# Graph attention in steps of four graphs: chunks attended to two slots sooner, and the last step projected in two halves

## The reference

```
h = jnp.maximum(_layernorm(x), 0.0)                 # x: 128 x 128 x 384
q, k, v = split_heads(h @ Wq + bq), split_heads(h @ Wk + bk), split_heads(h @ Wv + bv)
scores = einsum('bhqd,bhkd->bhqk', q, k) / sqrt(32) + beta * adj
scores = where(adj > 0, scores, -9e15)
out = x + einsum('bhqk,bhkd->bhqd', softmax(scores), v)
```

## Time and profile before

| | us |
|---|---|
| median of 3 runs | 978.81 (978.58 to 978.87) |
| the profiled execution's own time | 978.79 |
| its span, first to last instruction | 977.0 |
| PE busy | 953.0 (98% of the span) |
| ACT busy | 900.7 (92%) |
| DVE busy | 896.1 (92%) |
| POOL busy | 799.1 (82%) |

### The profile page before, as it was taken

How to read it: one execution, slowest core, us unless ns; L and a number is a source line. 1 busy time by engine, 2 the same in 40 slices (tenths; PEclk the granted TensorE clock), 3 DMA queues, 4 the chain that set the end, 5 groups by cost and what they waited for, 6 DMA issues and landing times.

```text
span 977.0 us, 33678 instructions
## 1 busy us (share of the span) xinstructions
PE 953.0 (98%) x10607; PEld 666.4 (68%) x10607; DVE 896.1 (92%) x4191; ACT 900.7 (92%) x2397; POOL 799.1 (82%) x998
## 2 busy tenths in 40 slices
PE   5999999999999999999999999999999999999995
PEld 2567667767667777667777667777667777667774
DVE  5899999999999999999999999999999999998887
ACT  7799999999999999999999999999999999999997
POOL 4798888888888888888888888888888888888762
PEclk9999999999999999999999999999999999999999
DMA  6799978998888989888998889999789998977941
GB/s 220 125 183 172 179 166 173 175 169 174 167 181 159 182 172 176 159 187 163 179 170 181 154 179 172 177 170 173 179 168 170 175 170 165 169 155 126 152 126 42
DMA packets 230933, 161.98 MB, mean 166 GB/s; under 512 B 106594, under 2 KB 230756, under 8 KB 230756
## 3 DMA queue, kind: packets, MB, share of 16 engines
q1 hardware_dynamic: 230480, 159.44, 86.3%
q10 hardware_dynamic: 276, 0.40, 0.1%
HBM read 35.52 MB, written 25.17 MB: 62 GB/s over the span
## 4 chain that ended last, share of the span: by engine, by line
PE 82%; issue 3%; POOL 2%; ACT 1%; DVE 1%; POOLq 0%; ACTq 0%; DVEq 0%
PE ps_p L529 49%; PE ps_t L549 15%; PE ps_s L541 8%; PE ps_o L565 3%; PE ps_o L566 3%; PE ps_o L564 3%; ACT probs L632 1%; POOL on L411 1%; DVE biased L764 0%; POOL weighted L387 0%; DVE pT L770 0%; POOL v L405 0%; POOL mask L391 0%; POOL rstd L365 0%; ACT pT L665 0%
## 5 line engine op out<-in xcount | busy, mean ns | idle before, releaser
L632 ACT ACTIVATE probs<-biased,neg_max 128x128 f32<-128x128 f32 x1536 | 490.9, 398 | 26.8 <-DVE neg_max L764 21.8
L529 PE MATMUL ps_p<-hT,w 128*128 128x512 f16 x1728 | 495.7, 379 | 0.2 <-POOL w L469 0.2
L764 DVE CUSTOM_DVE_ANT_0 biased<-ps_s,mask 128x128 f32<-128x128 f32 x1536 | 355.5, 287 | 48.3 <-PE ps_s L541 43.4
L770 DVE TENSOR_TENSOR pT<-ps_t,pT 128x512 f16<-128x512 f32 x384 | 263.5, 686 | 0.7 <-ACT pT L665 0.5
L529 PE MATMUL ps_p<-w,hT 128*128 128x384 f16 x1152 | 248.4, 325 | 0.2 <-POOL w L469 0.2
L549 PEld LDWEIGHTS ps_t<-ident,probs 128*128 128x128 f32 x1536 | 187.4, 140 | 75.5 <-ACT probs L632 22.0
L549 PE MATMUL ps_t<-ident,probs 128*128 128x128 f32 x1536 | 232.3, 274 | 5.5 <-ACT probs L632 5.3
L665 ACT ACTIVATE pT<-ps_t 128x512 f16<-128x512 f32 x384 | 224.5, 585 | 0.6 <-PE ps_o L566 0.6
L541 PEld LDWEIGHTS ps_s<-k_st,q_st 96*128 96x128 f16 x1536 | 117.1, 97 | 78.8 <-issue 1.9
L529 PEld LDWEIGHTS ps_p<-hT,w 128*128 128x128 f16 x1728 | 139.9, 97 | 33.8 <-POOL w L469 2.0
L564 PEld LDWEIGHTS ps_o<-v,pT 128*128 128x128 f16 x1536 | 132.4, 96 | 38.1 <-DVE pT L770 1.2
(11 more groups left out here) (76 smaller groups left out, 1157.8 us busy)
## 6 DMA issues: line engine op xcount, KB each, us to landing
q_st<-qT SPq DMA_DIRECT2D x288, 128.0 KB, 3.6
k_st<-kT SPq DMA_DIRECT2D x288, 128.0 KB, 4.8
out<-on SPq DMA_DIRECT2D x128, 192.0 KB, 3.5
xs<-in_x SPq DMA_DIRECT2D x31, 768.0 KB, 4.6
adjs<-in_adj SPq DMA_DIRECT2D x32, 256.0 KB, 5.5
hT<-h_parts SPq DMA_TRANSPOSE x60, 4.4
k_st<-in_L_gnn_Wk SPq DMA_DIRECT2D x1, 576.0 KB, 5.8
k_st<-in_L_gnn_Wq SPq DMA_DIRECT2D x1, 576.0 KB, 6.9
```

The lines of the kernel that those rows point to most:

```text
L529: mm = pe.matmul(dst, stationary, moving, start=m == 0, stop=m == MMS - 1)
L632: act.activation(probs[:, odd, i, :], biased[:, odd, i, :], ACT.Exp, bias=neg_max[:, odd, i:i + 1], scale=-1.0).then_inc(exp_done, 1)
L764: dve.tensor_tensor_reduce(out=biased[:, odd, i, :], in0=ps_s[:, i * N:(i + 1) * N], in1=mask[:, gp, v // CH, :], scale=-1.0, scalar=3.0e3 ...
L770: dve.tensor_tensor(pT[:, odd, 1], ps_t[odd][:].rearrange("p (h q) -> p h q", q=N), pT[:, odd, 0], ALU.subtract).then_inc(p_low_done, 1)
```

## The change

`LAG` goes from 0 to -2: the slot u of step s now attends to chunk u + 2 of the step before, and slots 10 and 11 to chunks 0 and 1 of their own step. The mask has to be there two slots sooner: POOL makes `weighted` before the last split of tokens and the mask right behind it. There is one transposing DMA for each graph (128 x 6 blocks x 128) in place of one for two. The statistics move one slot later on DVE, and the first sum over the squares of Wv one slot later on PE. The projections of step 31 go in two halves of two graphs (256 columns), spread evenly over 18 slots, so that they reach into step 32. The last graph's output is scaled and added on DVE, one chunk at a time, each from a PSUM bank of its own (`last_outputs`), and stored once.

```diff
-    LAG = 0
+    LAG = -2
...
+    LAST = STEPS - 1
+    HALF = G // 2
+    LAST_UNITS = [unit for g in (0, HALF) for unit in
+                  [("q", c) for c in range(CH)] + [("k", c) for c in range(CH)] + [("v", g + j) for j in range(HALF)]]
+
+    LAST_SLOTS = SLOTS + HALF * CH
...
         def chunk(s, par, u, behind):
 
-            v = u - LAG - behind
-            back = 2 if v < 0 else 1
-            n = SLOTS * (s - 1) + v
-            if v >= SLOTS or (not 0 <= n < CHUNKS):
+            ahead, v = divmod(u - LAG - behind, SLOTS)
+            g = s - 1 + ahead
+            if not 0 <= g < STEPS:
                 return None
-            return n, s - back, par if back == 2 else 1 - par, v % SLOTS
+            return SLOTS * g + v, g, g % 2, v
...
-            def turn_tokens(s, par, half):
-                rows = slice(G // 2 * half, G // 2 * (half + 1))
+            def turn_tokens(s, par, j):
                 wait(sp, proj_done, NB * (s - 1))
                 sp.nop(nofuse=True)
-                sp.wait_ge(h_low, G * (s - 2) + G // 2 * (half + 1))
+                sp.wait_ge(h_low, G * (s - 2) + j + 1)
                 sp.nop(nofuse=True)
-                sp.dma_start_transpose(hT[:, par, rows].rearrange("p j a c t -> p (j a c) t"),
-                                       h_parts[:, rows].rearrange("p j a d -> p (j a d)")).then_inc(hT_in, 16)
+                sp.dma_start_transpose(hT[:, par, j].rearrange("p a c t -> p (a c) t"),
+                                       h_parts[:, j].rearrange("p a d -> p (a d)")).then_inc(hT_in, 16)
...
-                if s == 0 and u in (8, 9):
...
-                ahead, j = {0: (2, 2), 1: (2, 3), 9: (3, 0), 10: (3, 1)}.get(u, (STEPS, 0))
+                ahead, j = {1: (2, 2), 2: (2, 3), 10: (3, 0), 11: (3, 1)}.get(u, (STEPS, 0))
...
+            def last_outputs(c):
+
+                g, j = LAST, G - 1
+                sums = ps_last[c][:, 0:HEADS * VW].rearrange("p (h d) -> p h d", d=VW)[:, c::CH]
+                inv = inv_sum[:, j % 2, c::CH]
+                part = on[:, j % 2, :].rearrange("p (h d) -> p h d", d=HD)[:, c::CH]
+                rest = xb[:, g % 2, j, :].rearrange("p (h d) -> p h d", d=HD)[:, c::CH]
+                dve.wait_ge(pv_done, CH * (G * g + j) + c + 1)
+                wait(dve, scaled, G * g + j - 1)
+                dve.reciprocal(inv, sums[:, :, HD]).then_inc(inverted, 1)
+                wait(dve, stored[j % 2], 16 * (G // 2 * g + j // 2))
+                dve.wait_ge(inverted, G * g + j + c + 1)
+                dve.tensor_tensor(part, sums[:, :, 0:HD], inv.rearrange("p (h o) -> p h o", o=1).broadcast_to([P, HPC, HD]),
+                                  ALU.mult).then_inc(last_scaled, 1)
+                dve.wait_ge(xb_done, G * g + j + 1)
+                dve.wait_ge(last_scaled, c + 1)
+                dve.tensor_tensor(part, part, rest, ALU.add).then_inc(last_added, 1)
```

More of the change, by code:

```diff
@@ L72, in bank_of, with units_of, tokens_of, turn_of @@
         return (NB * s + o) % PB
+    LAST = STEPS - 1
[3 more added lines that the diff above has]
+    LAST_SLOTS = SLOTS + HALF * CH
+    LAST_PIECES = [[] for _ in range(LAST_SLOTS)]
+    last_atoms = [(o, m, D if kind == "v" else HALF * N) for o, (kind, n) in enumerate(LAST_UNITS) for m in range(MMS)]
+    last_total = sum(a[2] for a in last_atoms)
+    done = 0
+    for o, m, cost in last_atoms:
+        runs = LAST_PIECES[(2 * done + cost) * LAST_SLOTS // (2 * last_total)]
+        if runs and runs[-1][0] == o:
+            runs[-1] = (o, runs[-1][1], m + 1)
+        else:
+            runs.append((o, m, m + 1))
+        done += cost
+    def units_of(s):
+        return LAST_UNITS if s == LAST else UNITS
+    def tokens_of(s, o):
+        if s < LAST:
+            return 0, G
+        return (0, HALF) if o < QK + HALF else (HALF, G)
+    def turn_of(s, o):
+        return o if s < LAST or o < QK else o - HALF
+    def pieces_of(s, u):
+        if s < LAST:
+            return s, PIECES[u]
+        slot = SLOTS * (s - LAST) + u
+        return LAST, LAST_PIECES[slot] if slot < LAST_SLOTS else []
+    def ended_in(s, u):
+        if u < 0:
+            s, u = s - 1, u + SLOTS
+        if s < 0:
+            return 0, []
+        of, runs = pieces_of(s, u)
+        return of, [o for o, a, b in runs if b == MMS]
     XB = 4
@@ L265, in _, with spread @@
                 sp.dma_start(xs[:, s], x_v[s]).then_inc(x_in[s], 16)
-            def spread(s, par, kind, c):
+            def spread(s, par, kind, c, half=0):
                 n, src, dst, landed = (0, qT, q_st, q_in) if kind == "q" else (1, kT, k_st, k_in)
@@ L300, in first_step, with last_steps @@
                 sp.dma_start(adjs[:], adj_v[1]).then_inc(adj_in, 16)
+            def last_steps(s, par):
+                if s == LAST:
+                    store(s - 2, 2)
+                    spread(s, par, "q", 0)
+                    spread(s, par, "q", 1)
+                    store(s - 2, 3)
+                    spread(s, par, "q", 2)
+                    for c in range(CH):
+                        spread(s, par, "k", c)
+                    store(s - 1, 0)
+                    store(s - 1, 1)
+                    spread(s, par, "q", 0, 1)
+                    spread(s, par, "q", 1, 1)
+                else:
+                    spread(s - 1, 1 - par, "q", 2, 1)
+                    store(s - 2, 2)
+                    for c in range(CH):
+                        spread(s - 1, 1 - par, "k", c, 1)
+                    store(s - 2, 3)
+                    for j in range(G):
+                        store(s - 1, j)
             def step(s, par):
@@ L370, in split_tokens @@
                 pool.wait_ge(normed, G * s + j + 1)
-                wait(pool, hT_in, 32 * (s - 2))
+                if s > 2:
+                    pool.wait_ge(hT_in, 16 * (G * (s - 3) + j + 1))
                 pool.nop(nofuse=True)
@@ L433, in step @@
                     add_x(s - 2, par, 3)
+                if s == STEPS:
+                    for j in range(HALF, G):
+                        split_v(LAST, 1 - par, j)
                 if masks:
@@ L493, in bank_free @@
                     return
-                before, last = divmod(NB * s + o - PB, NB)
-                kind, n = UNITS[last]
+                before, last = (s, o - PB) if o >= PB else (s - 1, NB + o - PB)
+                kind, n = units_of(before)[last]
                 if kind == "v":
@@ L498, in bank_free @@
                 else:
-                    pe.wait_ge(qk_low, QK * before + last + 1)
+                    pe.wait_ge(qk_low, QK * before + turn_of(before, last) + 1)
             def turn_first(s, bank, c):
@@ L592, in step @@
                         scores(*scored, (u - LAG) % 2)
-                    products = [(o, m) for o, first, end in (PIECES[u] if proj else []) for m in range(first, end)]
+                    of, runs = pieces_of(s, u)
+                    products = [(o, m) for o, first, end in runs for m in range(first, end)]
                     for o, m in products[:2]:
-                        project(s, par, o, m, m + 1)
+                        project(of, of % 2, o, m, m + 1)
                     if turning:
@@ L848, in step @@
                     scored, turned_late, valued = (chunk(s, par, u, behind) for behind in (0, 2, 3))
-                    ended = valued is not None and valued[3] % CH == CH - 1
+                    last = valued is not None and valued[1] == LAST and valued[3] // CH == G - 1
+                    ended = valued is not None and valued[3] % CH == CH - 1 and not last
                     if scored:
```

107 lines of the change are left out of this document (65 added, 42 removed).

## The result

The changed kernel takes 1082.26 us (median; 1077.21 to 1089.59), the kernel before, run beside it, 978.73 us (978.58 to 978.87): a ratio of 1.1064, 95% interval 1.0999 to 1.1128. It is 103.5 us slower, and the forecast was 974.7 us in a range of 969 to 990. The profiled execution took 1077.21 us, with a span of 1075.4.

The account below looks back on a forecast made before the run. It took PE, busy 98% of the span, to bound the kernel, leaving time in start, tail and waits. Terms +3.6 - 5.5 + 4.4 - 6.6 = -4.1 took 978.79 to 974.7 us, range 969 to 990.

Parts of the forecast that it names:

- term 3: Middle steps, SP and spread copies: scores wait 0.15 us a step for late k1 and k2, +4.4 us (range 0 to +16).
- k1 starts at 529.5, 1.8 us sooner: SP queue in step 17: with one half transpose of 0.7 us ahead, k1's spread copies start 1.8 us sooner.
- Nearer to the empty end: Spread wait chosen between 0.55 us a step and 0, nearer to 0 because the DMA queue seemed emptier: 0.15 us.
- second rival: Spreads become the bound: PE stands at slot 11 for 0.5 to 1.1 us a step, 985 to 1002 us; chance 0.22.
- The rule on the fixed part of a DMA: Spreads and transposes: about 2.0 us fixed per DMA would, in series, add two fixed parts a step; taken to overlap.
- Term 1: Start: PE waits for k0's last DMA until 38.4, chunk 2 at 43.0 in place of 39.37, +3.6 us (+2.0 to +5).
- Term 2: Middle steps, POOL: weighted made in idle time ends ACT's wait for v, 0.19 us in slot 0 over 29 steps, -5.5 us.
- Term 4: Last step in halves and tail: 18 slots of 2.1 us, 51.7 against 58.39 us, -6.6 us (-8.4 to -0.5).

Follow-up runs that it names:

- e5: The changed kernel with LAG = -1 in place of -2 and two whole transposes a step in place of four: 1002.86 us, ratio 1.0235.
- e1: The changed kernel, LAG -2 kept, with two transposing DMAs a step of two graphs each in place of four: 1083.88 us, ratio 1.1064.
- e2: The changed kernel with four output buffers in place of two, its four transposes kept: 1078.94 us, ratio 1.1013.
- e8: The changed kernel with two transposes a step, k1's copies ahead of the last transpose, k2's behind it, the store last, four output buffers: 1040.20 us, ratio 1.0623.
- e3: The changed kernel with LAG back at 0, all the rest kept, the four transposes too: 971.52 us, ratio 0.9924.
- e4: The changed kernel with LAG back at 0 and two whole transposes a step in place of four: 970.28 us, ratio 0.9911.
- e10: The changed kernel, but from step 2 on the second and third copy of each spread bring 4 tokens in place of 512: 1001.02 us, ratio 1.0219.
- e9: The changed kernel, but from step 2 on each unit's spread is one DMA in place of three, products still on 96 rows: 979.75 us, ratio 1.0008.
- e7: The kernel before with nothing but POOL's new order (weighted ahead of the last token split, mask right behind it): 972.35 us, ratio 0.9931.
- e11: e4 with POOL's old order, the moved statistics on DVE and moved sum on PE kept: 981.5 us, ratio 1.0025.
- e6: The changed kernel with only the first of three spread DMAs per q and k unit, and scores over 32 rows in place of 96: 1045.77 us, ratio 1.0681.

## Why the prediction was wrong, point by point

**The step that failed is term 3**, the spreads' wait: put at 0.15 us a step, or 4.4 us in all. A step went from 29.33 to 32.65 us, +3.3, where the changed POOL order should have taken 0.2 off. Two things in it were wrong.

- *"k1 starts at 529.5, 1.8 us sooner."* It started later. k1's issue stands 23.33 us into step 15 of the changed kernel (526.65 - 503.32), and stood 22.83 into step 17 (531.34 - 508.51); the means of steps 2 to 29 are 23.7 and 23.0. I had halved the transpose's 1.44 us to 0.7; the tile's rows, of the changed kernel and then of the kernel before, give

```profile
L339 SPq DMA_TRANSPOSE hT<-h_parts x120: 1220/1240/2456, 53.2 to 1011.8; - x120
```
```profile
L289 SPq DMA_TRANSPOSE hT<-h_parts x60: 1280/1438/2734, 52.1 to 909.9; - x60
```

  1.24 us for half the bytes. I also let k0 leave at its old place, though three transposes of 1.24 to 1.60 us now stand among the spreads ahead of it. k0 left 19.3 us into the step (522.61), where it left 18.1 into it before (526.62).
- *"Nearer to the empty end."* With k1 and k2 0.5 us later in place of 1.8 sooner, the same working comes near the result: k2's third DMA is issued at 534.58, 26.1 us into the step, plus 0.5, plus 4.1 to 5.7 to land, is 30.7 to 32.3, and slot 0 of the next step wants it at 29.3. That is 1.4 to 3.0 us late, and 3.3 were lost, of which up to 0.5 may be the clock. In the changed kernel it lands 32.25 us into the step on the mean of steps 2 to 29. The trace of before holds it in plainer form, if the tile `k_st` is read over 28 steps and not two: the third DMA of k1 lands 29.3 us after its step's start on the mean, that of k2 31.6, and with LAG -2 slot 11 and the next slot 0 want them at 26.9 and 29.3. Both would be 2.3 to 2.4 us late with their copies left where they were. (The expectation of e5 has 31.9 for k2.) The forecast hung on a gain of 1.8 us that no row showed. Neither theory that blamed the new placement (e1, e2) explains the loss. e8, the best order for SP that was tried, still lost 61 us.

My second rival had the mechanism (transposes keep most of their 1.44 us, PE stands at slot 11) and a price of 0.5 to 1.1 us a step, a third of the true one. The earlier trace rows were taken as a late and an early step, to be averaged; without the 1.8 us both are late.

**The rule on the fixed part of a DMA** (the Trainium skill, "DMA: Bandwidth & Descriptors", section "Anatomy of one DMA", about 2.0 us besides the bytes, fitted there to the gpsimd path, while SP issues these) was rightly not added up in series: twice the transposes cost 1.2 us at LAG 0 (e3 against e4) and at LAG -2 no gain from fewer is seen (e1), though the lower clock may hide one. But the bytes and above all the load of the queue do count. In e10 the two 1 KB copies of a unit of k landed in 2.3 and 1.9 us, near that fixed part, and in e9 full copies of 128 KB with little else in the queue in 3.0. In the changed kernel full ones took 4.4 (medians, 100 to 900 us). The 1.4 us between the last two come with the load, and they are what I treated as slack.

**Term 1, the start: +3.6 predicted, +3.6 measured** (38.47 for chunk 0, where 38.4 was put, and 43.01 for chunk 2, 43.0). But the account ended too soon. Step 1 takes 2.9 us more on top, of which about 2 are its own late spreads (in e9, whose step 1 still has all copies, slots 10 and 11 take 4.10 and 2.93).

**Term 2, POOL's order: -5.5 predicted, -6.9 measured by itself** (e7). Slot 0 went to 2.48 as said. At LAG -2 nothing of it is left in sum. Slot 0 does take 2.48 where no spread is late (e9), but slot 8 takes 2.61 in place of 2.43 in every step that normalises tokens, and 2.43 in step 30, which doesn't. ACT then has a k eviction and the normalisation just ahead of that slot's exponentials. That these cause it is argued from this pattern, not tested. What the working put at nothing, or at some 0.3 us a step without cover, was the moved statistics: 0.2 us a step without cover (e11), 0 with it (e4).

**Term 4, the last step and tail: -6.6 predicted**, -4.4 in the changed kernel and -5.8 in e9, where the last spreads are on time (the working's own numbers, 58.39 and 51.7, give -6.7). Slots of about 2.1 us were right (25.06 / 12 in step 31). In e9 the 18 slots and the three chunks behind them take 37.8 and 5.3 us, as said; the end takes 9.3 us after the last scores, where 8.6 was put. In the changed kernel one slot of step 32, ahead of chunk 6, which waits for the second half's spreads, takes 3.11 us in place of 1.94. At LAG 0 the same part gives 2.2 us (e4). The other 3.6 us are the two chunks done at the start, which cost 3.6 there. So the two slots sooner were a zero even on paper, and the working had this number in it (3.6 against what the tail gets back) without setting it beside the risk of term 3.

## What to carry to other kernels

When a consumer is moved ahead, first take, over many steps, how long after the step's start each of its inputs lands, and compare that with the new deadline. Only then look for what might make the inputs sooner, and count no such gain at full size unless a row shows it. Here the earlier start cost 3.6 us and the end gave 3.6 back, with PE full in between, so moving the stage forward could only have gained by removing a wait. The parts of a change should be priced apart: here POOL's order and the split last step gave 8.7 us together (e4), hidden under the 111 us that one constant cost.

## What the runs showed of the hardware that was not expected

- A transposing DMA of half the size holds SP for 1.24 us in place of 1.44, and lands 3.6 us after its issue in place of 4.4.
- The full 128 KB spreads landed up to 7.6 us after their issue in the changed kernel; before, up to 6.2.
- Score matmuls over 32 rows in place of 96 were no shorter (217 ns against 219), yet each of the kernel's slots became about 0.2 us longer. The group of their weight loads in e6, and the one in the kernel before:

```profile
L626 PEld LDWEIGHTS ps_s<-k_st,q_st 32*128 32x128 f16 x1536 | 84.9, 92 | 148.2 <-issue 145.9 <-DVE neg_max L856 2.3
```
```profile
L541 PEld LDWEIGHTS ps_s<-k_st,q_st 96*128 96x128 f16 x1536 | 117.1, 97 | 78.8 <-issue 1.9 <-DVE neg_max L764 1.6
```

  PEld's idle time ahead of them grew from 78.8 to 148.2 us, 0.045 us for each of 1536. Four a slot are 0.18 us, which is the 0.2. What this wait is stays open; e9, with 96 rows, doesn't have it.
- The load of the queue, more than a copy's own bytes, stretches the time to landing. Full copies of 128 KB took 4.4 us (median) at a DMA share of 0.88 and 3.0 at 0.45 (e9). In e10, at 0.48, the full first copy of a unit of k took 2.7 and the two of 1 KB behind it 2.3 and 1.9, so the bytes alone make 0.4 to 0.8 us.
- PE's granted clock fell to 0.50 for 3.41 us at 501.00, after 3.40 us in which PE was busy for 1.11.
